# One product of 200 columns in place of two of 100 in each block of a graph network's matrix build

## What is computed

```
edge_index = jnp.stack([src, dst])
h = max(layernorm(x), 0);  x = x + L0(h, edge_attr_2, ...)      # message network, mean over edges
h = max(layernorm(x), 0);  x = x + (h @ W1 + b1 + segment_sum(h[src], dst) @ W2 + b2)
h = max(layernorm(x), 0);  x = x + L2(h, edge_weight, W, bias)  # sum weighted by edge_weight and degrees
h = max(layernorm(x), 0);  x = x + (h + relu(0.9 * agg(h) + 0.1 * h))   # agg: sum weighted by degrees
```

## Time and profile before

| | |
|---|---|
| median of three runs | 1061.67 us (1057.26, 1061.67, 1062.37) |
| span of the profiled execution, first to last instruction | 958.9 us |
| time of the profiled execution itself | not listed on its page; the median run less the span is 102.8 us |
| instructions | 20,995, of them 7785 products and as many weight loads on PE |
| the sweep with gathers | from 75 us to 624 us of the span |

### The profile page before, as it was taken

How to read it: one execution, slowest core, us unless ns; L and a number is a source line. 1 busy time by engine, 2 the same in 40 slices (tenths; PEclk the granted TensorE clock), 3 DMA queues, 4 the chain that set the end, 5 groups by cost and what they waited for, 6 DMA issues and landing times.

```text
span 958.9 us, 20995 instructions
## 1 busy us (share of the span) xinstructions
PE 853.5 (89%) x7785; PEld 783.6 (82%) x7785; DVE 639.7 (67%) x1766; ACT 509.8 (53%) x1029; POOL 518.0 (54%) x477
## 2 busy tenths in 40 slices
PE   2445988888998788999999999998999999999997
PEld 2345978888998788899998999977889888888886
DVE  7607998787877877688888889858653311115664
ACT  3413765655766556677777777843443011114863
POOL 4177777777777877777777777753110000023110
PEclk9767999999999999999999999999999999999999
DMA  5672656556765586666566666664246888884500
GB/s 153 179 176 63 180 166 177 161 171 193 209 183 166 155 148 200 170 171 182 165 184 166 172 183 167 176 194 146 69 154 232 317 287 300 299 287 144 161 23 25
DMA packets 117410, 169.14 MB, mean 176 GB/s; under 512 B 17287, under 2 KB 83485, under 8 KB 117306
## 3 DMA queue, kind: packets, MB, share of 16 engines
q1 hardware_dynamic: 99834, 137.67, 45.0%
q0 software_dynamic: 13872, 28.32, 13.4%
q10 hardware_dynamic: 3600, 1.77, 0.6%
HBM read 109.26 MB, written 58.45 MB: 175 GB/s over the span
## 4 chain that ended last, share of the span: by engine, by line
PE 40%; POOL 34%; issue 10%; DMA 10%; DVE 3%; ACT 2%; SPq 1%; ACTq 0%; DVEq 0%
POOL room L766 33%; PE ps L1870 14%; PE ps L1855 14%; DMA room<-p_rows,idx 7%; PE ps L1694 3%; DMA edge_windows<-room 3%; PE ps L1695 2%; PE ps L1839 2%; PE ps L1728 1%; PE ps L1708 1%; PE ps L1639 1%; ACT h L872 1%; POOL pair L766 1%; DMA ST<-in_src 1%; PE ps L1668 1%
## 5 line engine op out<-in xcount | busy, mean ns | idle before, releaser
L766 POOL DMA_INDIRECT room<-p_rows,idx x416 | 440.4, 1059 | 144.6 <-issue 120.1
L1694 PE MATMUL ps<-room,ident 128*128 128x128 f32 x832 | 175.1, 293 | 61.7 <-DMA room<-p_rows,idx 60.1
L1694 PEld LDWEIGHTS ps<-room,ident 128*128 128x128 f32 x832 | 130.9, 198 | 70.7 <-DMA room<-p_rows,idx 50.9
L1728 PE MATMUL ps<-room 128*128 128x100 bf16 x2400 | 169.3, 207 | 0.0
L1695 PE MATMUL ps<-room 128*128 128x128 f32 x832 | 166.0, 282 | 0.0
L1284 DVE TENSOR_TENSOR room<-room,Wp 128x800 bf16<-128x800 bf16 x300 | 155.4, 572 | 0.0
L903 ACT ACTIVATE g<-ps 128x512 f32<-128x512 f32 x104 | 62.2, 598 | 170.9 <-PE ps L1695 169.4
L1726 PE MATMUL ps<-room 128*128 128x100 bf16 x800 | 151.7, 208 | 0.0
L1728 PEld LDWEIGHTS ps<-room 128*128 128x128 bf16 x2400 | 147.9, 97 | 3.5
L1870 PE MATMUL ps<-room,h 128*128 128x256 f32 (+1 forms) x650 | 136.2, 371 | 0.0
L1870 PEld LDWEIGHTS ps<-room,h 128*128 128x128 f32 x650 | 119.2, 190 | 15.2
(11 more groups left out here) (193 smaller groups left out, 1137.3 us busy)
## 6 DMA issues: line engine op xcount, KB each, us to landing
weight_blocks<-room SPq DMA_DIRECT2D x100, 400.0 KB
room<-weight_blocks SPq DMA_DIRECT2D x12, 3200.0 KB
room<-dst_row SPq DMA_DIRECT2D x104, 128.0 KB
room<-count_blocks SPq DMA_DIRECT2D x8, 1600.0 KB
count_blocks<-room SPq DMA_DIRECT2D x100, 100.0 KB
room<-p_rows,idx POOLq DMA_INDIRECT x416
first_c<-count_blocks SPq DMA_DIRECT2D x4, 1600.0 KB
edge_windows<-room SPq DMA_DIRECT2D x1, 3328.0 KB
```

What stands on the lines that cost most here:

```text
L766: return pool.indirect_dma_start(to, None, table, bass.IndirectOffsetOnAxis(ap=at, axis=0))
L1694: pe.matmul(to, ident[:, :], G[:, n % GS, c, :], start=True, stop=False)
L1728: weighed = pe.matmul(bank(6 + hh)[:, at], lo, movw[:, k, a, i, :, t], start=a == 0, stop=a == PARTS - 1)
```

## The change

In each block the counts and the first part of the weights become one product of 200 columns (`mov` and the first part lie in one tile now, so that they can be read as two runs of 100), and two products of 100 add the other parts onto its upper half. In PSUM a block has 256 columns, of which 100 are counts and 100 weights; a half of a step takes two neighbouring banks, 4 and 5 or 6 and 7. There is one semaphore for a half, raised by its last product.

```diff
-        mov_w = carve(SETS * NW * KCOLS)
-        movw_w = carve(SETS * PARTS * NW * KCOLS)
+        mov_w = carve(SETS * (1 + PARTS) * NW * KCOLS)
...
+        def block_out(hh):
+
+            return ps[:, 1024 * (2 + hh):1024 * (3 + hh)].rearrange("p (b c) -> p b c", b=NW)
...
             def read_blocks(u, hh):
-                act.wait_ge(s_cmm, 2 * u + hh + 1)
+                act.wait_ge(s_wmm, 2 * u + hh + 1)
...
-                act.wait_ge(s_wmm, 2 * u + hh + 1)
...
                 for a in range(PARTS):
-                    last = dve.tensor_tensor(movw[:, k, a, :, :, :], mov[:, k, :, :, :],
+                    last = dve.tensor_tensor(mov[:, k, 1 + a, :, :, :], mov[:, k, 0, :, :, :],
                                              blocks_of(Wp[:, a, :], u, KCOLS), ALU.mult)
...
-                    at = slice(KCOLS * b, KCOLS * b + KCOLS)
-                    lo = sta[:, k, i, :, t]
-                    counted = pe.matmul(bank(4 + hh)[:, at], lo, mov[:, k, i, :, t], start=True, stop=True)
-                    for a in range(PARTS):
-                        weighed = pe.matmul(bank(6 + hh)[:, at], lo, movw[:, k, a, i, :, t],
-                                            start=a == 0, stop=a == PARTS - 1)
-                counted.then_inc(s_cmm, 1)
+                    lo, to = sta[:, k, i, :, t], block_out(hh)[:, b, 0:2 * KCOLS]
+                    pe.matmul(to.rearrange("p (a c) -> p a c", a=2), lo, mov[:, k, 0:2, i, :, t], start=True, stop=False)
+                    for a in range(1, PARTS):
+                        weighed = pe.matmul(to[:, KCOLS:2 * KCOLS], lo, mov[:, k, 1 + a, i, :, t],
+                                            start=False, stop=a == PARTS - 1)
                 weighed.then_inc(s_wmm, 1)
```

More of the change, by code:

```diff
@@ L210, in gnn_kernel @@
         lg = g3_flat[:, RS * 4 * D + 128:RS * 4 * D + 128 + 32 * GROUPS].rearrange("p (g e) -> p g e", g=GROUPS)
-        mov = mov_w.bitcast(bf16).rearrange("p (s i c t) -> p s i c t", s=SETS, i=NW, t=2)
-        movw = movw_w.bitcast(bf16).rearrange("p (s a i c t) -> p s a i c t", s=SETS, a=PARTS, i=NW, t=2)
+        mov = mov_w.bitcast(bf16).rearrange("p (s a i c t) -> p s a i c t", s=SETS, a=1 + PARTS, i=NW, t=2)
         sta = sta_w.bitcast(bf16).rearrange("p (s i n t) -> p s i n t", s=SETS, i=NW, t=2)
@@ L361, in gnn_kernel @@
         s_bop = sem("block_operands")
-        s_cmm = sem("counts_in_psum")
         s_cev = sem("counts_read")
@@ L917, in window_rows, with half_of @@
                                bias=onesr[0:WIN, 0:1]).then_inc(s_sT, 1)
-            def halves_of(of, hh):
-                return (bank(of + hh, NW * KCOLS).rearrange("p (b h w) -> p b h w", b=NW, w=4),
-                        slice(16 * hh, 16 * hh + 16))
+            def half_of(weighed, hh):
+                cols_of = block_out(hh)[:, :, KCOLS * weighed:KCOLS * weighed + KCOLS]
+                return cols_of.rearrange("p b (h w) -> p b h w", w=4), slice(16 * hh, 16 * hh + 16)
             def read_blocks(u, hh):
-                act.wait_ge(s_cmm, 2 * u + hh + 1)
+                act.wait_ge(s_wmm, 2 * u + hh + 1)
                 if u >= OUTS and hh == 0:
                     act.wait_ge(s_cst[u % OUTS], 16 * (u // OUTS))
-                of, at16 = halves_of(4, hh)
+                of, at16 = half_of(0, hh)
                 act.activation(cnt_out[:, u % OUTS, :, at16].rearrange("p h (b w) -> p b h w", w=4), of, ACT.Copy)\
                     .then_inc(s_cev, 1)
-                act.wait_ge(s_wmm, 2 * u + hh + 1)
                 if u >= OUTS and hh == 0:
                     act.wait_ge(s_wst[u % OUTS], 16 * (u // OUTS))
-                of, at16 = halves_of(6, hh)
+                of, at16 = half_of(1, hh)
                 act.activation(w_out[:, u % OUTS, :, at16].rearrange("p h (b w) -> p b h w", w=4), of, ACT.Copy)\
@@ L1276, in block_operands @@
                 k = u % SETS
-                link(dve.tensor_tensor(mov[:, k, :, :, :],
+                link(dve.tensor_tensor(mov[:, k, 0, :, :, :],
                                        iota_k[:, :, :].rearrange("p (a c) t -> p a c t", a=1)
```

## The result

| | before | after |
|---|---|---|
| median | 1059.41 us (1054.26 to 1062.96, 18 runs) | 1052.09 us (1047.66 to 1062.33, 18 runs) |
| profiled execution: span | 958.9 us | 1047.0 us |
| profiled execution: its own time | not listed | 1048.83 us |
| instructions | 20,995 | 19,299 |

The ratio is 0.9945, with a 95% interval of 0.9924 to 0.9966: the change makes the kernel faster by some 6 us.

The account below looks back on a forecast made before the run. The prediction took POOL's gathers to bound the sweep, with PE second by a small margin. Span 958.9 − 0.07 = 958.8 us, plus 102.8 us around it, gave 1061.6 us, no change, range 1056.0 to 1067.0.

Parts of the forecast that it names:

- the ground of the sum: Whole kernel: a span of 958.8 us after the change, with 102.8 us around it, giving 1061.6 us.
- POOL as the bound: Sweep: POOL issues gathers back to back, about 5.4 us a quad, and waits for nobody; PE is second by 10.5 us.
- the 0 for PE's gain in the sweep: Sweep: PE's saved time only lengthens its wait for the next gather; only 16 groups behind the last landing gain, −0.07 us.
- The prediction's own sign for this: POOL's waits: waits for line 1695 of a microsecond and more would mean that PE bounds the sweep.
- The group of products: Blocks on PE: one wide and two narrow products take 179.4 ns, saving 4.3 ns a group, 3.4 us in 800 groups.
- The product of 200 columns: Blocks on PE: forecast 87.6 ns; the rival had it stream slowly, 77 ns more a group, 1083.4 us, chance 0.05.
- ACT's reads: ACT's reads over two banks: forecast no cost at about 500 ns; the rival had them double, 1087 us, chance 0.02.
- the collisions: POOL's gathers in the sweep: rival that shifted overlaps with DVE move the time, 1057.0 or 1066.3 us, chance 0.14.
- The weight loads: PE: forecast at no cost; the rival had 97 ns a load set the pace, 1060.1 us, chance 0.06.

Follow-up runs that it names:

- before profiled again: The kernel before with no edit, profiled a second time: 1053.39 us with a span of 1051.5 us.
- the kernel with the narrow product: The kernel before with the third weight product of each block on 2 columns in place of 100: 1060.24 us, ratio 0.9992.
- The kernel with the two products of 100: The changed kernel with each product of 200 columns made as two of 100, layout, semaphore and reads kept: 1062.32 us, 1.0024 of the kernel before.
- the ones with more and fewer instructions elsewhere: The kernel before with three met waits more ahead of each block on PE, 1.0073; with one gather product for four in `pre`, 0.9938.
- the waits on SP: The kernel before with 16 or 48 met waits more in each of 100 steps on SP: 1079.42 and 1098.94 us, against 1070.72.

## Why the prediction was wrong, point by point

**The step that failed is the ground of the sum: "958.9 − 0.07 = 958.8 us of span. Around the span lie 102.8 us if the profiled execution took as long as the median run".** As far as the other runs tell, it had not. In after 1.8 us lie around the span (1048.83 − 1047.0), in before profiled again 1.9 (1053.39 − 1051.5). By that, the 102.8 us were some 100 us of the sweep that the trace did not have. The condition was written down, and nothing was made of it: no rival asked what the other 100 us would be. A fixed price around a span should have looked too large by itself. The Trainium skill ("Runtime: NRT & Kernel Launch", section "The ~15µs preamble/postamble breakdown") has some 9 to 15 us for what is done ahead of and behind a kernel; the 1.8 us here are below that, and 102.8 far above.

**POOL as the bound, and with it the 0 for PE's gain in the sweep.** "In the sweep PE's gain only lengthens its wait for the next gather: 0" follows from POOL as the bound. That was read from the first trace, and in the main rightly, though even there POOL's gathers have 39.6% of the chain over 500 to 625 us, and PE's lines 1694, 1695, 1728 and 1708 have 28.3%. For the executions that were timed it is wrong: POOL has at most 1% of the chain in each of the fourteen other traces, and the term put at 0 measured −5.8 us. The prediction's own sign for this, POOL waiting for PE by a microsecond and more, is in the waits above (1.7 us and, where the releaser isn't known, 2.3).

**The group of products** was right: 179.4 ns forecast, 0.18 us in the chain. The 4.3 ns for a product that goes were put at −3.4 us of PE's work and held to be hidden; that this is near the 5.8 us is no merit of the sum, since 15 us less of PE's work brought nothing in the kernel with the narrow product. The product of 200 columns has 0.09 us in the chain, so it doesn't stream slowly, and that rival falls.

**ACT's reads** were right at no cost: 502 and 505 ns. That rival falls too. **The gathers** have a mean of 1028 ns in after and 994 in before profiled again, one trace each, so the collisions did not decide: the faster kernel has the slower gathers.

**The weight loads** as a pace: the chain has a group of three products at 0.18 us, 60 ns each with a load of its own, so that the 97 ns of a load are not on the path; the rival falls by size. Whether a load counts for more or less than another instruction no run separates: each product that went took one with it.

**What held in place of the sum**: the change takes 1696 instructions out of the sweep (800 products, 800 loads, 96 waits on ACT), and in the timed executions the time follows the number of instructions. The kernel with the two products of 100, the one with two columns, the ones with more and fewer instructions elsewhere, and the waits on SP show this. That it does so by way of the stops is likely and not shown. With the change the breaks of over 0.25 us within the blocks fall from 203 to 50 and from 121 us to 32, but `pre` and `seg` have more of them: all of PE's "issue" rows add up to 92 us in the trace of after and to 92 in that of the kernel before profiled again.

What the stops are is open. Three things bear on it. They are absent in one execution of the same program with the same 20,995 instructions, so the program alone does not make them. Each timed run of after lists a span, so each was recorded, and an instruction more on any engine would be a record more. The Trainium skill ("NOTIFIC — the notification-queue block", sections 7.1 and 10) says that the block that writes such records holds on the order of 500 of them and holds the producers back when its inside is full, though it also calls a record free for the engine at 6.6 million a second. Here some 25 instructions start in a microsecond of the sweep (15,043 in 590 us), 25 million a second. By that the stops would be the price of being recorded, and a run that isn't recorded would not have them. Against it stands the first trace, which is a record too: there 16,624 instructions start in the same 590 us, and no such break lies in the blocks. No run here was without records, and instruction supply would also count every instruction, so it stays a reading and not a finding. In an execution without stops, as in the first trace, the prediction's sum may still hold; no run shows it.

## What to carry to other kernels

Before a trace is read for what bounds a kernel, its span has to be set against the times to be forecast: where they are a tenth apart, as here, a second profile shows whether that much lies around a span, or whether the trace is of an execution of another kind, whose bound doesn't carry over. Where a profile shows "issue" in the midst of a run of products and the other engines start nothing either, count instructions, on all engines: fewer and wider ones gained here though the columns stayed the same (5.8 us for 1696), and waits that are always met were not free (8.7 to 12.9 ns each).

## What was not expected of the hardware

All engines of the core stop together, while transfers go on: some 200 breaks within the blocks in one sweep, 121 us of 590, at no semaphore that the profile shows. 78,400 columns less on PE, some 15 us of its work, moved the time by less than can be measured (0.9992 [0.9965, 1.002]), while 800 waits on an engine off the chain cost 10.3 us.
